# Attention outputs of a fused transformer layer: scaled to unit mean square before they are turned, turned by DMA in 16-bit halves, projected in 16 bits

## The reference, cut to what matters

```python
p = p1 - lam * p2                       # two causal softmax maps
o = jnp.einsum('bqhk,bkhe->bqhe', p, v) # 256 columns for each head pair
rms = jax.lax.rsqrt(jnp.mean(o * o, axis=-1, keepdims=True) + EPS)
o = o * rms * subln_w
o = o * (1.0 - LAMBDA_INIT)
return o.reshape(B, S, H * D) @ out_w.T + out_b
```

## Time and profile before

| | us |
|---|---|
| median of 3 runs | 1295.33 |
| lowest, highest | 1293.17, 1296.08 |
| the profiled execution, its own time | 1293.83 |
| its span, first to last instruction | 1292.0 |

### The profile page before, as it was taken

The page is one execution under the profiler, slowest core; times in us unless marked ns, Lnnn a source line. Parts: engine busy times, 40 slices in busy tenths (PEclk is TensorE's granted clock), DMA queues, the critical chain, the costliest instruction groups (busy, mean ns, idle before and its releaser), DMA issues.

```text
span 1292.0 us, 26833 instructions
## 1 busy us (share of the span) xinstructions
PE 1232.1 (95%) x8350; PEld 1071.9 (83%) x8350; DVE 998.0 (77%) x2488; ACT 1069.4 (83%) x2818; POOL 732.4 (57%) x1038
## 2 busy tenths in 40 slices
PE   8899999999999999999999999999996897998998
PEld 6788888888988888889888888788875785886887
DVE  6888888887788788878788878786888789537545
ACT  5889999998799999978899989897888889845341
POOL 3466566554655665637565555465597556565532
PEclk9999999999999999999999999999997999998999
DMA  3244443434354444332643354334333352510001
GB/s 127 64 69 81 74 79 71 87 58 74 52 110 70 73 68 83 66 65 47 105 81 68 71 81 82 67 50 102 67 81 66 60 91 42 131 36 1 29 18 37
DMA packets 298522, 89.86 MB, mean 70 GB/s; under 512 B 289680, under 2 KB 296080, under 8 KB 297872
## 3 DMA queue, kind: packets, MB, share of 16 engines
q1 hardware_dynamic: 297040, 86.58, 35.7%
q10 hardware_dynamic: 1344, 1.57, 0.3%
HBM read 14.71 MB, written 2.10 MB: 13 GB/s over the span
## 4 chain that ended last, share of the span: by engine, by line
PE 67%; DVE 8%; ACT 8%; POOL 7%; issue 5%; DMA 5%; ACTq 0%; SPq 0%; POOLq 0%; DVEq 0%
PE score_bank L993 8%; PE score_bank L999 7%; PE score_bank L996 7%; PE score_bank L1133 7%; DMA p16T<-p 4%; POOL e_all L1687 3%; ACT e_all L1172 3%; PE turn_bank L1098 3%; PE turn_bank L1020 2%; PE turn_bank L1021 2%; PE turn_bank L1022 2%; PE turn_bank L1079 2%; DVE p L1412 2%; PE sum_bank L1020 2%; PE sum_bank L1021 2%
## 5 line engine op out<-in xcount | busy, mean ns | idle before, releaser
L1687 POOL TENSOR_TENSOR e_all<-e_all 128x512 f32<-128x512 f32 (+3 forms) x320 | 373.6, 1188 | 105.2 <-ACT e_all L1187 104.7
L1172 ACT ACTIVATE e_all<-score_bank,negmx 128x512 f32<-128x512 f32 (+2 forms) x640 | 398.7, 635 | 31.9 <-DMA p16T<-p 17.8
L1401 DVE TENSOR_REDUCE mx<-score_bank 128x1 f32<-128x512 f32 (+1 forms) x384 | 243.4, 639 | 46.1 <-PE score_bank L999 43.7
L993 PE MATMUL score_bank<-k_hi,q_hi 128*128 128x512 f32 (+2 forms) x640 | 253.6, 396 | 20.2 <-ACT e_all L1172 13.3
L1412 DVE SCALAR_TENSOR_TENSOR p<-e_all,gain,p 128x512 f16<-128x512 f32 (+3 forms) x320 | 259.5, 826 | 16.1 <-ACT p L1194 15.1
L996 PE MATMUL score_bank<-k_lo,q_hi 128*128 128x512 f32 (+2 forms) x640 | 232.9, 364 | 0.4 <-DVE k_lo L1456 0.4
L999 PE MATMUL score_bank<-k_hi,q_lo 128*128 128x512 f32 (+2 forms) x640 | 232.8, 364 | 0.0
L1194 ACT ACTIVATE p<-e_all,gain 128x512 f16<-128x512 f32 (+3 forms) x320 | 206.7, 673 | 16.5 <-POOL e_all L1687 15.7
L1187 ACT ACTIVATE e_all<-e_all,ratio 128x512 f32<-128x512 f32 (+3 forms) x320 | 198.0, 668 | 10.2 <-POOL ratio L1675 9.8
L993 PEld LDWEIGHTS score_bank<-k_hi,q_hi 128*128 128x128 f32 x640 | 121.5, 190 | 54.8 <-issue 21.0
L1675 POOL TENSOR_SCALAR ratio<-s,inv,neg_lam 128x1 f32<-128x1 f32 x128 | 54.8, 428 | 149.9 <-DVE inv L1666 145.8
(11 more groups left out here) (389 smaller groups left out, 3049.9 us busy)
## 6 DMA issues: line engine op xcount, KB each, us to landing
p16T<-p SPq DMA_TRANSPOSE x320, 3.0
w_raw<-in_w_qkv_dram SPq DMA_DIRECT2D x3, 1024.0 KB, 6.1
w_raw<-in_w_o_dram SPq DMA_DIRECT2D x4, 512.0 KB, 3.4
w_raw<-in_w_ug_dram SPq DMA_DIRECT2D x4, 512.0 KB, 3.8
bv<-in_hidden_dram SPq DMA_DIRECT2D x8, 256.0 KB, 3.0
out_dram<-e SPq DMA_DIRECT2D x16, 128.0 KB, 1.7
e<-in_w_d_dram SPq DMA_DIRECT2D x1, 1024.0 KB, 6.5
x_in<-in_hidden_dram SPq DMA_DIRECT2D x2, 256.0 KB, 3.7
```

Of the source, the lines that this page charges most:

```text
L993: pe.matmul(bank[:, 0:w], qh, kh, start=True, stop=False)
L1172: act.activation(e, S[k % NS][:, 0:w], ACT.Exp, bias=negmx[:, d % 2, m, s:s + 1], scale=-1.0 if alone else 1.0, accum_out=ssum[:, d % 4, s ...
L1401: dve.tensor_reduce(mx[:, d % 2, m, s, c:c + 1], S[k % NS][:, 0:w], X, ALU.max)\
L1687: pool.tensor_tensor(a, a, b, ALU.add).then_inc(p_pool, 1)
```

## The change

Outputs are normed before they are turned. For each output, after the last PV:

- SQ on ACT squares the work bank itself, divided by 2048 before the square; the copy to o_sum is gone.
- VE on DVE adds epsilon; OT on POOL is now the power alone.
- OH on ACT writes the bank times rms as the 16-bit high half into o16, OL on DVE the low half.
- OX on SP turns the four 128x128 blocks of o16 by one DMA transpose into oT16; the turn on PE is gone.
- OP projects with six 16-bit matmuls; DVE adds the result times a factor of the group (out_unit).

The work bank stays taken until OL has read it. The weights of the output projection are now 16-bit halves too. So that they fill the 16-bit range, each group has a new bound: OQ on ACT squares the raw weights (four instructions), OV on PE sums over partitions, OS on DVE and POOL makes the factors. WO waits for that.

The factors of a tile (GAIN) move from POOL to DVE, as two instructions behind the reciprocal. Scaling the e2 chunk (E2) is done by whichever of ACT and POOL comes to it first in the plan: of the 320 chunks POOL gets 123 (62 of 512 columns, 47 of 384, 9 of 256, 5 of 128), ACT 197. On ACT its rank falls from 2 to 3.

The diff, cut to its core (the steps of the bound and the allocation of tiles are left out):

```diff
-                    add("G", "POOL", "GAIN", o, 0.54, [("DVE", "INV", o)] + ([] if o else [("DVE", "LAM2", None)]), 0)
+                    add("I", "DVE", "GAIN", o, 0.16, [("DVE", "INV", o)] + ([] if o else [("DVE", "LAM2", None)]), 0)
...
-                        add("A", "ACT", "E2", (d, jj), 0.19 + 0.00083 * ww, [("POOL", "GAIN", o)], 2)
-                        add("M", "POOL", "MIX", (d, jj), 0.19 + 0.00212 * ww, [("ACT", "E2", (d, jj))], 2)
+                        add("A", "ACT", "E2", (d, jj), 0.19 + 0.00083 * ww, [("DVE", "GAIN", o)], 3)
+                        add("M", "POOL", "MIX", (d, jj), 0.19 + 0.00212 * ww, [("DVE", "GAIN", o)], 2)
...
-                add("P", "ACT", "PV", o, 0.27, [pe] + ([("PE", "OT", o - 2), ("ACT", "SQ", o - 2)] if o >= 2 else []), 0)
-        elif kind == "OT":
-            add("O", "ACT", "OT", what, 0.27, [pe] + ([("PE", "OP", what - 2)] if what >= 2 else []), 0)
-            add("R", "ACT", "SQ", what, 0.40, [pe], 1)
-            add("N", "POOL", "OT", what, 0.9, [("ACT", "SQ", what)] + ([("DVE", "OP", what - 4)] if what >= 4 else []), 0)
-            add("O", "DVE", "OT", what, 0.34, [("ACT", "OT", what)], 1)
+                add("P", "ACT", "SQ", o, 0.40, [pe] + ([("DVE", "VE", o - 4)] if o >= 4 else []), 0)
+                add("N", "DVE", "VE", o, 0.08, [("ACT", "SQ", o)], 0)
+                add("N", "POOL", "OT", o, 0.55, [("DVE", "VE", o)] + ([("DVE", "OL", o - 4)] if o >= 4 else []), 0)
+                add("R", "ACT", "OH", o, 0.29, [("POOL", "OT", o)] + ([("SP", "OX", o - 4)] if o >= 4 else []), 0)
+                add("R", "DVE", "OL", o, 0.4, [("ACT", "OH", o)], 0)
+                add("X", "SP", "OX", o, 1.2, [("DVE", "OL", o)] + ([("PE", "OP", o - 4)] if o >= 4 else []), 0, 2.2)
...
+        if op.kind == "E2":
+            scaling.add(op.what)
+        if op.kind == "MIX":
+            mixed.add(op.what)
+            if op.what not in scaling:
+                orders[engine].insert(-1, ("E2", op.what))
+                us += 0.32 + 0.00085 * duo_chunks(op.what[0])[op.what[1]][4]
...
+                        sp.dma_start_transpose(oT16[:, o % 4, :].rearrange("p (b n) -> p b n", n=P), o16[:, o % 4, :])\
+                          .then_inc(turned_o[o % 4], 16)
...
-                            mm = pe.transpose(bank[:, et * P:(et + 1) * P],
-                                              o_sum[:, what % 2, et * P:(et + 1) * P], ident[:, :])
-                        mm.then_inc(t_full, 1)
...
-                        pe.wait_ge(t_hi, t_use["OT", o] + 1)
...
+                        pe.wait_ge(turned_o[o % 4], 16 * (o // 4 + 1))
+                        if o % (2 * DUOS) < 2:
...
-                                mm = pe.matmul(bank[:, 0:HID], a[:, o % 2, et * P:(et + 1) * P],
-                                               w[:, s, et, :], start=(n == 0), stop=(n == 5))
+                                at = (CT * a + et) * P
+                                mm = pe.matmul(bank[:, 0:HID], oT16[:, o % 4, at:at + P], wo16[:, s, et, w, :],
+                                               start=(n == 0), stop=(n == 5))
...
-                        act.activation(o_sum[:, o % 2, :], bank_for(kind, o)[:, 0:HID], ACT.Copy).then_inc(o_ready, 1)
...
-                        act.activation(oT_hi[:, o % 2, :], bank_for(kind, o)[:, 0:HID],
-                                       ACT.Copy).then_inc(t_hi, 1)
...
-                        act.activation(o_half[:, o % 2, :], o_sum[:, o % 2, :], ACT.Square,
-                                       scale=float(2 * D) ** -0.5, accum_out=msq[:, o % 4:o % 4 + 1])\
+                        act.activation(o_half[:, o % 2, :], bank_for("PV", o)[:, 0:HID], ACT.Square,
+                                       scale=float(2 * D) ** -0.5 / O_UNIT, accum_out=msq[:, o % 4:o % 4 + 1])\
                            .then_inc(msq_ready, 1)
+                    elif kind == "OH":
+                        o = what
+                        act.wait_ge(rms_ready, o + 1)
+                        if o >= 4:
+                            act.wait_ge(turned_o[o % 4], 16 * (o // 4))
+                        act.activation(o16[:, o % 4, 0:HID], bank_for("PV", o)[:, 0:HID], ACT.Copy,
+                                       scale=rms[:, o % 4:o % 4 + 1]).then_inc(o_hi, 1)
...
+                        dve.scalar_tensor_tensor(out=o16[:, o % 4, HID:2 * HID], in0=bank_for("PV", o)[:, 0:HID],
+                                                 scalar=rms[:, o % 4:o % 4 + 1], in1=o16[:, o % 4, 0:HID],
+                                                 op0=ALU.mult, op1=ALU.subtract).then_inc(o_lo, 1)
...
-                                                 scalar=rms[:, o % 4:o % 4 + 1], in1=so_far,
+                                                 scalar=out_unit[:, o // (2 * DUOS):o // (2 * DUOS) + 1], in1=so_far,
...
+                        dve.tensor_scalar(rms_b[:, c], msq[:, c], eps_v[:, g:g + 1], None, ALU.add).then_inc(rms_step, 1)
...
+                    elif kind == "GAIN":
+                        o = what
+                        d, s = o // 2, tile_of(o)[0]
+                        dve.wait_ge(ratio_step, o + 1)
+                        if o == 0:
+                            dve.wait_ge(lam_step, 2)
+                            dve.wait_ge(lam_ready, 2)
+                        if d >= 4:
+                            dve.wait_ge(p_lo, CHUNKS * (d - 3))
+                        dve.scalar_tensor_tensor(out=ratio[:, d % 4, s:s + 1], in0=s12[:, d % 4, s, 0:1],
+                                                 scalar=inv[:, d % 4, s, 1:2], in1=neg_lam[:, 0:1],
+                                                 op0=ALU.mult, op1=ALU.mult).then_inc(ratio_ready, 1)
+                        dve.tensor_scalar(gain[:, d % 4, s:s + 1], inv[:, d % 4, s, 0:1], full[:, 0:1], None,
+                                          ALU.mult).then_inc(gain_ready, 1)
 
...
+                    if kind == "E2":
+                        d, j = what
+                        o, s, _, _, w, _ = duo_chunks(d)[j]
+                        e = e2_of(CHUNKS * d + j, w)
+                        pool.wait_ge(ratio_ready, o + 1)
+                        pool.tensor_scalar(e, e, ratio[:, d % 4, s:s + 1], 0.0, ALU.mult, ALU.add).then_inc(e2_scaled, 1)
```

More of the change, by code:

```diff
@@ L422, in needs @@
             return [("DVE", "CV", what)]
+        if kind == "OV":
+            return [("ACT", "OQ", what)]
         if kind == "F":
@@ L486, in start @@
     def start(engine):
+        for line in (waiting.get(("ACT", "A"), ()),):
+            while line and line[0][1].what in mixed:
+                line.popleft()
         heads = [line[0] for (e, _), line in waiting.items() if e == engine and line]
-        heads = [(op.rank, n, op) for n, op in heads if all(x in done for x in op.after)]
+        heads = [(op.rank, n, op) for n, op in heads if all(x in done for x in op.after)
+                 and not (op.kind == "MIX" and op.what in scaling and ("ACT", "E2", op.what) not in done)]
         if not heads:
```

215 lines of the change are left out of this document (125 added, 90 removed), and 6 rows, old and new, of the table FIRST_STEPS.

## The result

The change takes **1284.15 us** (median of 4 runs, 1282.03 to 1285.9) where the kernel before, on the same chip, takes 1295.7 us (4 runs, 1293.17 to 1298.37). The ratio is 0.991, 95% interval 0.9882 to 0.9938: 11.7 us faster, between 8 and 15. The forecast was 1270: the sign and the range held, and of the 24 to 25 us of gain less than half came.

What follows compares the result with a forecast made beforehand. PE was taken as the bound from 60 to 960 us (883 of 900 busy). From 1293.83 us, -34.2 (PE) + 3 (short stretch) + 6 (late maxima) + 1 (attention's end) gave 1269.6, stated as 1270; range 1252 to 1290.

Steps and rivals of the forecast that it cites:

- in the long stretch the end moves with the work of PE: From 60 to 960 us PE is busy 883 of 900 us, so time off PE there shortens the run.
- That buys nothing by itself, since PE is the bound: ACT getting 112 us lighter was left out of the sum and kept only for the range.
- PE's work: Turn off PE 28.2 us, 16-bit projection 6.4 us, new bound's matmuls 0.4 us back: 34.2 us off PE.
- it doesn't do what it says: Rival: PE's freed time turns into idle time because p arrives no sooner; no change in time, chance 0.04.
- ACT, -112 forecast: On ACT two copies an output go (99.3 us) and 123 scalings leave (82.2); OH adds 62.3 us, OQ 7.0.
- POOL, -49 forecast: On POOL 131.3 us go; 123 scalings at 0.61 us add 76 us, the new bound 7 us; hidden either way.
- between nothing and all 28: Charge of 6 us for waits on maxima that come late, as DVE gets 67.0 us more and its cover thins.
- The rival on DVE: DVE becomes the bound through late maxima if it cannot hold 87.8% over 60 to 960 us; chance 0.15.
- The DMA turn: 128 output transposes join SP's queue of 320, 1.23 us each to issue, landing at median 3.0 us.
- The place named: End of the attention, where 6.2 us of other steps cover a 5 to 9 us path to the projection; 1 us charged.
- the rival with 0.27 us an output: Projections wait for the DMA; at 0.27 us of waiting an output the gain is gone; chance 0.09.
- The rule on the subtractions: DVE subtractions reading two SBUF tiles and POOL's SBUF reads exclude each other: some 10 us longer, end 3 us later.

Runs made afterwards that it cites:

- The run with four matmuls: Kernel before, its projection making four of six matmuls (products with the output's low half left out): ratio 0.9931 to the kernel before, 8.9 us saved.
- the run with the steps back on POOL: Changed kernel with epsilon and both factors of a tile on POOL again, order planned anew: median 1274.11 us, ratio 0.9824 to the kernel before.
- moving the load: Changed kernel with the 1 MB load of the down projection's weights issued behind the last output's turn: ratio 0.9881 to the kernel before.
- a version with 18 us less on DVE: Apparently the changed kernel with epsilon alone added by POOL again, order planned anew: ratio 0.9944 to the kernel before, 7.3 us saved.

## Why the prediction came out as it did

**The step that failed** is the first: "in the long stretch the end moves with the work of PE". The run with four matmuls gives 0.3 us for each us off PE (0.46 at the most, with the edit's own waits given back), in the kernel before. Its sister, "That buys nothing by itself, since PE is the bound", failed as well: 47 busy us off ACT gave 10.2. I read 883 busy of 900 us as a bound. The work of the four other queues is chained to PE's by banks and buffers in a fixed order (score, maximum, exponential, factor, addition, split, turn, PV), and the end moves with the chain, which passes from engine to engine. The page gave a sign of it: only 67% of the chain was on PE.

**The sum with measured prices**, an estimate from these runs: PE 34 x 0.3 = -10; ACT 74 x 0.22 = -16; DVE +11; the DMA path +7. That gives -8, and 11.7 off was measured (8.0 to 15.3). But the prices are not firm: with 0.46 PE's term is -16, and with the 0.08 that ACT's load cost in the change itself (all scalings on ACT) its term is -6, so the sum lies anywhere from -14 to +2. The measured time is consistent with it and does not confirm it. What the runs do show is that the forecast was not one term too large but wrongly composed: PE's term two to three times too large, ACT's missing, DVE's and the DMA's too small. That the time still fell in the range is in part luck: ACT's relief, counted for nothing, made up for some of what was missing.

- *PE's work.* The size was right: six 16-bit matmuls of the projection take 0.65 us from start to start in the trace after (615.82 to 616.47), 0.66 was taken, and no turn is left. What was wrong is that it counts one for one. The rival "it doesn't do what it says", given 0.04, describes most of it: PE's freed time turned into idle time, 20 us of it in the long stretch.
- *ACT, -112 forecast, -74 measured.* I added lengths. The lengths of ACT's groups add up to 1358 us before, for 1069 us of busy time, since the next activation starts before the last has ended. They fell by 134 and the busy time by 74. The Trainium skill says the same ("Perfetto Trace Analysis", Optimizing Scalar/DVE Operations): part of an instruction's profiled length overlaps the next instruction; the rows agree. OH was right (0.475 to 0.481 us, 0.487 taken).
- *POOL, -49 forecast, -32 measured.* The scaling of 512 columns takes 0.774 us, mean 0.728, where 0.61 was taken between 0.483 and 1.328.
- *DVE.* Its busy time was right to 1 us, in part by luck: the three steps were priced by the length of one instruction, 0.154 us, where their own lengths are 0.205 to 0.294, and the 6.7 us of longer subtractions (below) were not in the 67. Its price was charged at 6 us "between nothing and all 28"; it is 11 by the run with the steps back on POOL. The rival on DVE had the right sign of evidence (waits on maxima and on exponentials both grew), but not its rule, that DVE decides only from 87.8% of the stretch: in the kernel before, far below, 43 us more already cost 7.
- *The DMA turn.* The landing was shorter than taken (median 2.5 us, 3.0 taken). The path costs 7 us where 1 us was charged. The place named, the end of the attention, holds its longest wait, but moving the load brought 2 to 4 us back, not clear of noise. Elsewhere projections waited three times, 1.2 us at the most, so the rival with 0.27 us an output fell.
- *The rule on the subtractions* was given 10 us more. Their busy time rose by 6.7 us in all (259.5 to 266.2), the 512-column form from 0.901 to 0.919 us. Means hide what happens, and single instructions show it. Two places of after, DVE and POOL:

```profile
439.13 0.74 DVE L1452 SCALAR_TENSOR_TENSOR p<-e_all,gain,p 128x512 f16<-128x512 f32 x1
...
428.17 2.21 DVE L1452 SCALAR_TENSOR_TENSOR p<-e_all,gain,p 128x512 f16<-128x512 f32 x2
...
428.51 1.33 POOL L1749 TENSOR_TENSOR e_all<-e_all 128x384 f32<-128x384 f32 x1
```

  A subtraction of 512 columns with no POOL instruction beside it takes 0.74 us (65 of 160 in after, 47 in before, each between 0.725 and 0.753), which is what the one that reads a bank takes (0.744). In the second place the latter of two starts while POOL adds, and takes 1.50 us. The longest takes 1.83. The one of 256 columns that reads a bank and one SBUF tile (L1448 before, L1482 after) has the same mean, 0.475 to 0.478 us, with and without wide POOL work beside it. The Trainium skill's rule ("SBUF — State Buffer", Who interferes with whom) says that a VectorE instruction with two SBUF inputs and a GpSimd one that reads SBUF exclude each other. The traces agree, by up to 1.1 us an instruction. Summed over the 320 subtractions, what they take above their undisturbed length is 52.5 us before and 59.2 after (an estimate by the median of the undisturbed ones of each size). But POOL's additions cause most of it (42 and 49 us), and these are 320 in both kernels; the new scalings on POOL account for 2. So the mechanism was right, and its size does not go with POOL's busy time: with all scalings on ACT, 83 us less on POOL, the 512-column form still takes 0.918 us and all 320 take 263.3.

**What stays open:** how the price of a us on one engine depends on the load of the others. Three prices for DVE (0.16 and 0.5 for load added, 0.19 for load taken off) and three for ACT (0.22, 0.08, near zero) were measured, besides a version with 18 us less on DVE that was not faster, and no rule gives them.

## What to carry to other kernels

An engine that is busy for 98% is not yet the bound in a kernel whose engines hand work round in a fixed order: here a us off PE gave 0.3, at most 0.46. Its part of the chain of waits is a warning and not a price: PE with 67% gave 0.3, ACT with 8% gave 0.22. To know the price, relieve the engine alone and time it. Before you pay for relief on the fullest engine with load on another, put that load alone into the old kernel and time it. Price what an engine gains or loses in busy time, not in summed lengths, which overlap. Where a mean length is longer than a like instruction's, look at single instructions and at what runs beside them. And ask of each moved step what its queue does while the step waits for its input.

## What the hardware showed that was not expected

- A DVE instruction of one column with a factor read from memory for each partition is 205 ns long (294 with three inputs) where one with a constant has 154; in busy time the three of an output cost 0.154 us each in the mean.
- A DVE subtraction of two SBUF tiles that starts while POOL adds two others is held up: 0.74 us alone, up to 1.83 beside it, 52 us over the run before and 59 after.
- Lengths of neighbouring instructions overlap by so much that they add up to 127% of ACT's busy time (1358 of 1069 us) and 113% of DVE's (1124 of 998).
- Behind one pause of PE of 3.8 us the granted clock fell from 1.00 to a mean of 0.78 in the window from 1125 to 1130 us; with the load moved, and a pause of 1.9 us, it stayed at 1.00.
